# An AdaLN-style stack of two routed feed-forwards and an attention: normalising the outputs one head pair later, and fetching routed rows one pair earlier

## The reference, cut to what matters

```python
x = x + ffn_b(ffn_a(x, cond))                       # two routed feed-forwards, 8 experts, top 2
x = x + ffn_d(attention(x, bias, mask, cond))       # 16 experts, top 2, and a shared one

def attention(x):                                   # one batch element, 16 heads of 64, one shared key/value head
    xn  = layernorm(x) * g_in
    q   = xn @ Wq;  k, v = split(xn @ Wkv)          # one null key and value in front
    p   = softmax(q @ k.T / 8 + bias, causal and masked)
    out = (p @ v) @ Wo
    return layernorm(out) * g_out

def ffn_d(z):                                       # for every row: two of 16 experts
    scores = sigmoid(z @ gate_w.T);  pick top 2 of (logits + expert_bias)
    ...
```

## Time and profile before

| | us |
|---|---|
| median of 3 runs | 742.62 |
| lowest and highest | 741.37, 742.75 |
| the profiled execution, its own time | 741.12 |
| its span in the trace | 738.1 |
| TensorE busy | 680.2 (92%) |
| VectorE busy | 476.3 (65%) |
| ScalarE busy | 390.7 (53%) |
| GpSimd busy | 434.0 (59%) |

### The profile page before, as it was taken

One profiled execution on the slowest core, in us unless ns is written; L12 is line 12 of the kernel. 1 busy time (PEld: TensorE's weight loads), 2 busy tenths in 40 slices (PEclk: granted clock), 3 DMA queues, 4 the chain that ended last, 5 costly groups with the idle time before them and its releaser, 6 DMA issues. The chain is left out here.

```text
span 738.1 us, 15562 instructions
## 1 busy us (share of the span) xinstructions
PE 680.2 (92%) x4353; PEld 531.6 (72%) x4354; DVE 476.3 (65%) x1732; ACT 390.7 (53%) x1091; POOL 434.0 (59%) x556
## 2 busy tenths in 40 slices
PE   7889989857999999977999998999999998999996
PEld 4469976646999999964666666667666654688885
DVE  0834466665544454327787988899988946277646
ACT  4566622336444444316776667676766625677611
POOL 1077507715555863247767798899897645166650
PEclk9999999966999999999999999999999999999998
DMA  9936634573887775523899999898988773587738
GB/s 329 344 95 190 167 107 136 146 261 90 228 232 223 212 218 167 189 80 134 300 321 351 331 338 356 274 314 281 311 264 303 265 268 153 149 247 239 227 114 307
DMA packets 126860, 170.93 MB, mean 232 GB/s; under 512 B 30272, under 2 KB 101952, under 8 KB 125888
## 3 DMA queue, kind: packets, MB, share of 16 engines
q1 hardware_dynamic: 109680, 132.37, 54.6%
q0 software_dynamic: 10944, 30.03, 13.2%
q10 hardware_dynamic: 6160, 7.64, 3.1%
HBM read 102.42 MB, written 67.57 MB: 230 GB/s over the span
## 5 line engine op out<-in xcount | busy, mean ns | idle before, releaser
L1927 ACT ACTIVATE work<-work 128x129 f32<-128x129 f32 (+1 forms) x256 | 114.4, 448 | 69.6 <-DVE work L2058 68.7
L2083 DVE STREAM_TRANSPOSE region_bd<-work 128x384 f32<-128x384 f32 x128 | 73.0, 570 | 13.6 <-DMA c_blocks<-region_bd 9.2
L1673 PE MATMUL psY<-work,region_ac 128*128 128x256 f32 x256 | 70.0, 396 | 3.6 <-ACT work L1921 3.6
L1478 POOL DMA_INDIRECT d_pairs<-work,home x47 | 47.1, 1003 | 42.4 <-DVE work L1189 33.0
L2368 POOL TENSOR_TENSOR work<-region_bd,region_ac 128x386 f32<-128x386 f32 x64 | 59.3, 937 | 17.8 <-DVE work L2058 10.0
L1467 POOL DMA_INDIRECT b_pairs<-work,home x39 | 38.0, 974 | 52.2 <-DVE work L1147 50.8
L2368 POOL TENSOR_TENSOR work<-work,region_ac 128x386 f32<-128x386 f32 x64 | 59.2, 941 | 16.0 <-DVE work L2058 8.4
L1711 PE MATMUL psM<-region_ac,work 128*128 128x256 f32 x256 | 66.9, 384 | 0.0
L1105 ACT ACTIVATE work<-work 128x512 f32<-128x512 f32 x39 | 24.6, 630 | 75.7 <-DVE work L1138 75.7
L1459 POOL DMA_INDIRECT work<-in_x,inv x39 | 37.1, 951 | 45.3 <-DVE inv L1377 33.7
L925 PE MATMUL psH<-work,region_bd 128*128 128x128 f32 x472 | 58.1, 276 | 4.1 <-DMA work<-d_turned 3.0
(11 more groups left out here) (393 smaller groups left out, 1622.2 us busy)
## 6 DMA issues: line engine op xcount, KB each, us to landing
c_blocks<-region_bd SPq DMA_DIRECT2D x64, 512.0 KB, 4.2
region_bd<-c_blocks SPq DMA_DIRECT2D x64, 512.0 KB, 5.1
work<-d_rows SPq DMA_DIRECT2D x47, 132.0 KB, 2.7
a_slots<-work SPq DMA_DIRECT2D x19, 256.0 KB
b_turned<-work SPq DMA_DIRECT2D x35, 128.0 KB, 2.9
work<-b_turned SPq DMA_DIRECT2D x35, 128.0 KB
region_bd<-in_b_w SPq DMA_DIRECT2D x1, 3072.0 KB, 21.5
region_ac<-in_fside SPq DMA_DIRECT2D x12, 256.0 KB
```

The source lines that it names most:

```text
L1478: pool.indirect_dma_start(out=st.pair_dram, out_offset=bass.IndirectOffsetOnAxis(ap=home[:, t:t + 1], axis=0), in_=d_ys[:, t % ROWS, :], i ...
L1673: last = pe.matmul(psY[:, 0:SEQ], c_wq[:, c, j * P:(j + 1) * P], c_xnT[:, odd, c, :], start=(c == 0), stop=(c == KD - 1))
L1927: nc.scalar.activation(c_p[:, j % 2, o, a:z], c_sc[:, o, a:z], ACT.Exp, scale=-1.0, bias=c_min[:, o, i:i + 1], accum_out=c_sum[:, j % 2, o ...
L2083: nc.vector.transpose(out=c_x1[:, p % 2, :, (QT + 1) * o:(QT + 1) * (o + 1), :].rearrange("p b i q -> p i b q"), in_=c_p[:, j % 2, o, 1:1 ...
```

## The change

Six edits, all of order; no operation is added or removed, and TensorE's and SyncE's orders stay as they were.

1. Start of stage B, ScalarE: the copy of the first tile's rows stands behind the first three weight copies, not behind the first.
2. VectorE: statistics of the outputs at the end of step 6, not 5 (in the last batch step 7, as before).
3. GpSimd: `pool_out_rstd` at step 7 after the first `bm` (before: step 6 after the second).
4. ScalarE: `act_out` at the end of step 7, behind the second half's exponentials.
5. GpSimd: `pool_z` and `pool_z_again` in step 0 of the next batch, behind the first `bm` and the pairs' work there (before: step 7 behind the second `bm`). What the last batch itself finishes stays where it was.
6. ScalarE: `act_load_pairs` at the end of step 2, not 3.

```diff
@@ act_ffn_b
-            place_w(0, 0)
+            for o in range(RING - 1):
+                place_w(0, o)
             copy_x(0)
-            place_w(0, 1)
-            place_w(0, 2)
@@ act_batch
-                if j == 7 and not first and not last:
-                    act_out(act, b - 1)
@@
-                if j == 3 and b + 2 < BATCH:
+                if j == 2 and b + 2 < BATCH:
                     act_load_pairs(act, b + 2)
@@
                 if j == 7 and last:
                     act_shared_halves(act, 2, 3)
+                if j == 7 and not first:
                     act_out(act, b - 1)
@@ dve_batch
-                if j == (7 if last else 5) and not first:
+                if j == (7 if last else 6) and not first:
@@ pool_batch
-                    if (j, n) == ((7, 0) if last else (6, 1)) and not first:
+                    if (j, n) == (7, 0) and not first:
                         pool_out_rstd(pool, b - 1)
-                    if j == 7 and n == 1 and not first:
+                    if j == 0 and n == 0 and b >= 2:
+                        pool.wait_ge(C.z_step, 2 * b - 2)
+                        pool_z(pool, b - 2)
+                        pool_z_again(pool, b - 2)
+                    if j == 7 and n == 1 and last:
```

## The result

| | before | changed |
|---|---|---|
| median of 6 runs each, one chip, us | 743.15 (741.37 to 744.5) | 749.63 (743.67 to 753.45) |
| ratio, 95% interval | | 1.0091 (1.0054 to 1.0127) |
| the same pair once more (e13 below), 29 and 6 runs | 741.07 | 749.99, ratio 1.0105 (1.0071 to 1.0139) |
| profiled execution and its span | 741.12, 738.1 | 743.67, 741.9 |

The account below looks back on a forecast made before the run. TensorE was taken to set the pace in attention. +1.65 (last batch) + 1.2 (earlier boundaries) - 0.5 (pair loads) = +2.35 us on 742.62 gave 745.0 us, range 741.2 to 747.6.

Parts of the forecast that it names:

- the output path: Late normalised outputs and z turns in attention: +1.65 us at the last batch plus 1.2 us at earlier boundaries.
- The last batch, +1.65: Third pair of the last batch: second bm ends behind late pool_z, VectorE's scores begin at 568.9, not 567.19; +1.65 us.
- The statistics, 0: VectorE's output statistics, at most 1.15 us, move from step 5 to step 6; taken as zero cost.
- The pair loads, -0.5: Loads one step earlier ease TensorE's wait for blocks in batch 3: gain between 0 and 1.72 us, -0.5 taken.
- The boundaries of batches 3, 4 and 5, +1.2: VectorE's scores begin 0.5 us later at each boundary; sum 1.2 us, between 0 and 1.5.
- the 0.5 passes on in full: Batches 4 and 6, where TensorE already waited for VectorE: full 0.5 us delay; in batch 5 between 0 and 0.5.
- Rival D: Statistics find VectorE full in step 6, step 7 begins 1.15 us later: 749.6 in full, 747.3 at half; chance 0.17.
- gain near zero: Pair loads, by the rule that DMA engines serve queues in turn: almost no gain, the sum 0.5 us higher.
- Stage B, 0: Start of stage B: three weight copies end 1.5 us before the turned rows arrive; nothing gained or lost.
- 2.6 us of delay: End of step 7, batch 6: normalising ends at 565.5 instead of 562.9, behind the second half's exponentials.
- Rival B: Pair loads' gain is whole, TensorE's three waits for blocks go, -2.9 us: 742.6, no change; chance 0.2.
- C: VectorE, without statistics in step 5, catches up into step 7; only the loads' gain is left: about 740.9; chance 0.13.

Follow-up runs that it names:

- e13: The whole change run again beside the kernel before, on one chip: 749.99 us, ratio 1.0105.
- e4: Kernel before with only the output path's edits 3, 4 and 5: 745.4 us, ratio 1.0057.
- e9: Kernel before with only edits 3, 4 and 5, run again on another chip: 746.37 us, ratio 1.0065.
- e14: Whole change with edit 4 undone, so the normalised outputs stay early: 741.77 us, ratio 1.0002 to the kernel before.
- e1: Kernel before with only the pair loads moved to step 2 (edit 6): 745.75 us, ratio 1.0083.
- e2: Whole change with edit 6 undone, pair loads back at step 3: 749.2 us, ratio 1.0107 to the kernel before.
- e10: Kernel before with only the normalised outputs late (edit 4), z turns still in step 7: 757.92 us, ratio 1.0212.
- e3: Kernel before with only edit 1, the start of stage B; attention unchanged: 742.27 us, ratio 1.0023.
- e15: Kernel before with only the z turns (pool_z, pool_z_again) moved behind the next batch's first bm (edit 5): 735.66 us, ratio 0.9929.
- e5: Edits 3, 4 and 5 on the kernel before, but z turns behind the second bm of step 0: ratio 0.9975 to the kernel before.
- e8: As e1, but each early pair load moves only 64 of 256 values of one half (output wrong): ratio 0.9952 to the kernel before.
- e6: Kernel before with only the z turns moved behind the next batch's first bm (edit 5), first run: ratio 0.9955.
- e16: Kernel before with only the pair loads split, first row's at step 2 and second row's at step 3: ratio 0.999.

## Why the prediction was wrong

The sign was right and the size was not: 6.5 us where 2.35 were forecast. 0.5 us of the 4.6 by which the time was missed is the starting point, since the kernel before came out at 743.15 over six runs, not 742.62. **The step that failed first is the price of the late normalised outputs.** The sum put 2.85 us on the output path, 1.65 at the last batch and 1.2 at three boundaries; 4.2 and 4.8 us were measured for it alone (e4, e9, by their ratios), and undoing the move of the two normalising instructions in the whole change takes away 8.2 us (e13 against e14). Two more terms failed beside it, the statistics at 0 and the pair loads at -0.5. Step by step:

- **The last batch, +1.65.** Right in mechanism and place. Against TensorE's turning of the staged rows the scores begin 1.55 us later, TensorE's wait is 1.93 in place of 0.39, and the stretch is 1.86 us longer in the profile of the changed kernel. But that profile is of the fastest of six executions. Seven profiled kernels had a TensorE wait of 1.3 us or more at this gate product (the changed kernel, e1, e2, e4, e9, e10, e13). In six of them the granted clock fell in the 10 us that follow, and their last stretch was 2.5 to 4.7 us longer than that of before. In the thirteen others the wait was 0.64 or less and the clock stayed at 1.00 there. The sum priced a stall of TensorE at its length and had no term for this. Where a wait of 1.94 us was followed by a fall (e2, e13, e4, e9), the last stretch was 1.1 to 2.8 us longer than in the changed kernel's own profile, with the same wait and no fall.
- **The boundaries of batches 3, 4 and 5, +1.2.** Mis-sized. The three intervals are 1.46, 0.73 and 0.98 us longer, 3.2 in all, and 4.8 in e13. The first of them tells little, since e3 has it 1.86 us longer with attention unchanged. The other two are clear: 1.7 us and 2.6 us (e13) where 0.75 was forecast, and shorter than before with the outputs early (e14). VectorE's waits went from 1.39 to 1.68 and 1.82, as forecast. What failed is the bound: "the 0.5 passes on in full" took TensorE's waits of before as the only way down, and put 0 to 0.5 on the rest. The late moments that GpSimd now waits for come just ahead of the same boundaries; what part they have was not tried.
- **The statistics, 0.** Wrong: alone, with the deviations behind them, +0.46% (3.6 us of 782). Rival D, with 0.17 of the chance, had the direction. With the outputs early and the z turns late, though, the same statistics leave no loss that can be told (e14).
- **The pair loads, -0.5.** Wrong in sign: alone +0.83%. The forecast saw what would happen ("loads that start a step earlier slow an earlier write instead") and still took a gain. The write of 444.77 took 7.8 us, that of 450.10 had taken 8.0. From the rule of the Trainium skill, "DMA: Bandwidth & Descriptors", section "Queues, rings and completion order", by which the queues are served in turn, the forecast had drawn a gain near zero. That was nearer than its term, and no run here shows the turns themselves. In the whole change the loads add nothing that can be told (1.0105 and 1.0107 with and without).
- **Stage B, 0.** Nothing shown against it; the interval reaches from -0.1 to +0.6%.
- **What the sum lumped.** Edits 4 and 5 were priced as one move. Apart, edit 5 gains 0.5 to 0.7% (one `bm` fills GpSimd's idle time ahead of `pool_z`, and in e15's profile TensorE no longer waits for VectorE) and edit 4 costs 2.1%. The forecast's 2.6 us of delay less 0.9 us of work moved ahead was right arithmetic for the pair, but hid that one half of the change was worth keeping.

Rival B fails (TensorE's wait for blocks in batch 3 is 2.62, not below 0.3), and so does C: the kernel is slower, not faster. One reading was loose: "a batch takes about 32.2 us" fits the two later intervals, but the one of batch 3 took 34.80, and 2.81 of the 35 us of the first stretch in the earlier trace rows are idle.

How the loss divides between late work and the clock is known only roughly. The estimate used above, span times one minus the mean granted clock, averaged over all runs of a kernel and set against the kernel before, gives for the clock 3.7 us in e1, 3.3 in e4, 1.7 in e9, 3.5 in e2 and 0.9 in e13, each with an uncertainty of 1.6 to 2.3 us. So the clock can be half of e1's 6 us; in the whole change it may be anything from none to half.

Something else stays open. The parts do not add up: loads, statistics and z turns, each alone at +0.83, +0.46 and -0.71%, make 1.0002 together (e14), where 1.006 would be the sum. That a VectorE idle for a landed write loses nothing by having its statistics moved away from there would fit, but was not tried. VectorE's wait for landed writes is no price by itself: in e15, the fastest kernel of the four that ran together, it is 15.4 us in all, as long as e1's 15.8 and longer than the 9.2 of before.

## What to carry to other kernels

On an engine that works in order, do not ask what a moved piece of work costs but what stands behind it when its input is late: the same z turns changed the time by -0.5 to -0.7% with their input ready and by +0.6% with it up to 3.3 us late, and moving them behind one more 0.9 us instruction brought that back. Price a producer's move and a consumer's move apart, even where a change makes both. And where a change stalls the critical TensorE, look whether the clock falls behind the stall, over several executions, and look for the same wait and fall in a kernel that lacks the change: here one profile of the changed kernel missed the fall at the gate product, and showed another one that the unchanged order has too.

## What the runs showed of the hardware

- TensorE's granted clock fell from the 2.4 GHz to the 1.2 GHz level inside an otherwise full attention stage, and not each time: after stalls of 1.3 to 2.9 us at the last batch's gate product in six profiles of seven, in batch 3 after stalls of 2.75 us (e3) and 2.88 us (e1), but not after one of 2.57 us in batch 3 of e14. In e9 two stretches of 5 us in a row ran at 0.66. The last stretch took 62.11, 62.97, 63.07 and 63.84 us where a stall of 1.94 us was followed by a fall (e2, e13, e4, e9), against 61.03 with the same stall and no fall.
- In one set of runs (e5 to e8) everything ahead of attention took some 28 us more (first turn at 356 to 359 us instead of 326 to 330, the kernel before at 782.33 us), while attention took what it took elsewhere: 278.65 us in e6 there, 281.79 in e15. These runs and e13 to e16, which took the usual time, carry the same chip number, so whether this belongs to a chip is not shown. The ratios of the same kernel in both sets agreed within 0.3% (e6 and e15).
- A 512 KB write that starts about 2 to 3 us behind two loads of 256 KB takes longer: until the read behind it was let go, 5.9 to 8.0 us passed at six such places in the kernel before, 5.1 to 7.8 in the changed one, where it is another write, and 3.9 to 5.8 in e8, whose loads have hardly any bytes. The median to landing of all these writes is 4.2 us.
